# Where GpSimd pauses between scatters, the last tiles of a loop, and four smaller edits in a graph network of four layers

## The chip, the cores and the metric

The kernel runs on one NeuronCore of a Trainium2 chip. The metric is the device time of one execution in microseconds (us). Three executions of the kernel before took 2736.61, 2769.08 and 2771.64 us, median 2769.08. The profiled execution took 2730.27 us, with a span of 2728.6 us from the first to the last instruction.

## The reference, cut to what matters

3125 nodes with 256 features, 103125 edges sorted by target node. Four graph layers follow one another, each on the layer norm of the sum so far:

```python
h = relu(layernorm(x)); x = x + L0(h)   # out-degree scaled sums over src of t1[src] + (feat[src]*feat[dst]) @ W2, then norm
h = relu(layernorm(x)); x = x + L1(h)   # weighted, normalised adjacency, then a 2-layer MLP
h = relu(layernorm(x)); x = x + L2(h)   # undirected adjacency, then a norm over all nodes
h = relu(layernorm(x)); x = x + L3(h)   # attention with 4 heads, softmax over the edges of a target
```

All four use the same edges. So the kernel first builds dense matrices of 25 by 25 blocks of 128 by 128 cells: in one the number of edges between two nodes, in the other their summed weight.

## The kernel before

**Edges.** Each of the 806 columns of an edge list of 128 by 806 is written by one indirect DMA of GpSimd (L378, a scatter of 128 cells) into `table` in HBM. Two edges that fall on the same cell must be merged first. VectorE and TensorE do this in `dedupe(c)` for a batch of 128 columns at a time, seven batches (0 to 6); a batch runs eight passes of an equality test (L452), a weighting (L458) and matmuls with an identity that sum them (L800). The code of every batch is written out; it is not shared between batches. Between batch 1 and batch 2 the same two engines count degrees: `onehot` (L534 to L538) and `degrees` in a loop of 31 groups. Scatter c waits for its batch (`cols`), and the first 160 for the clearing of the part of `table` that they fall in. From scatter 304 (`CALM`) on, a memset of GpSimd on 128 columns of `rest` (L377) stands in front of each scatter.

**L0 and L1's gathering.** When all seven batches are done, 25 steps follow (`step`, L585, L751, L871), one per tile of 128 target nodes. SyncE loads the tile's cells from `table` (L333) once the scatters that fall in it are done (`need`, `done`), TensorE turns and multiplies them, VectorE and ScalarE finish the tile's L0 and its L1 contribution. `overlapped` (L71) orders the steps: tile 0 by itself, then a hardware loop (`Fori`) whose body holds two steps, then the last tiles written out: for the last but three `step` as in the loop, for the last but two without turning the next tile (`more=False`), for the last but one with the earlier tile's gathering ahead of its own loads (`ahead=True`), and the last. L624 runs once in each step.

**L1's rest and L2.** `phase_l12` first does L1's MLP. Then it goes over seven groups `g` of target tiles: 4, 4, 4, 4, 4, 4 and 1. Each group has five parts of 20 matmuls (L1180, shown as L1098); a matmul is as wide as the group's columns: 512, or 54 for the last group.

**L3.** `l3_fast` starts with three `Exp` on ScalarE (L1882 to L1884), the first behind a table load. TensorE spreads two rows with 28 matmuls (L1977), ScalarE copies each row (L1888), VectorE starts once both are there (L1952). GpSimd scales the 25 tiles of `ftx` (L1876), and TensorE's first pass waits for each. The rest of the kernel is L3's eight passes (L2015).

**At the start** five loads bring `src`, `dst` and `dst` shifted by 1, 64 and 512 edges; `extremes` (L419) runs behind batch 0's passes.

Of the kernel before, what the change touches and what calls it, by code (L numbers as in the profile page):

```python
# [37 lines left out]
CALM = 304  # L38
# [32 lines left out]
def overlapped(eng, step):  # L71

    assert NT % 2
    m = NT // 2
    step((0, 0, 0), None)
    with eng.Fori(0, m - 2) as i:
        step((2 * i + 1, 1, i), (2 * i, 0))
        step((2 * i + 2, 0, i + 1), (2 * i + 1, 1))
    step((NT - 4, 1, m - 2), (NT - 5, 0))
    step((NT - 3, 0, m - 1), (NT - 4, 1), more=False)  # L80
    step((NT - 2, 1, m - 1), (NT - 3, 0), ahead=True)
    step((NT - 1, 0, m), (NT - 2, 1), last=True)
    step(None, (NT - 1, 0))
# [101 lines left out]
def phase_edges_and_l0(nc, sem, sb, a):  # L185
# [7 lines left out]
    with ctx:  # L193
# [3 lines left out]
        def pieces(flat, *shapes):  # L197
# [18 lines left out]
        srci, dsti, dst1, dst64, dst512, key, fl, sent, red = pieces(  # L216
            region[:, :, :].rearrange("p a n -> p (a n)"), (I32, EC), (I32, EC), (I32, EC), (I32, EC), (I32, EC),
            (F32, EC), (F32, 3, EC), (F32, EC), (F32, 3, P))
        t0, t1, f0 = fl[:, 0, :].bitcast(I32), fl[:, 1, :].bitcast(I32), fl[:, 2, :]
# [39 lines left out]
        rest = buf("rest", [P, P])  # L259
# [22 lines left out]
        def _(eng):  # L282
            rows = lambda t: t.rearrange("(p c) -> p c", p=P)
            for t, s in ((srci, a.src[0:EP]), (dsti, a.dst[0:EP])):
                eng.dma_start(t, rows(s)).then_inc(sem("ld"), 16)
            for t, s in ((dst1, a.dst[1:EP + 1]), (dst64, a.dst[SH:SH + EP]), (dst512, a.dst[LONG * SH:LONG * SH + EP])):
                eng.dma_start(t, rows(s)).then_inc(sem("ldr"), 16)
# [54 lines left out]
        def _(eng):  # L342
# [20 lines left out]
            late = 20  # L363
            for g in range(NGS):
# [20 lines left out]
        def _(eng):  # L385
# [8 lines left out]
            eng.wait_ge(sem("ldr"), 48)  # L394
# [46 lines left out]
            def dedupe(c):  # L441
# [28 lines left out]
                if c == 0:  # L470
                    extremes()
                if c == 0:
                    eng.wait_ge(sem("ldm"), 64)
# [20 lines left out]
                eng.sem_inc(sem("cols"), 1)  # L494
            dedupe(0)
# [89 lines left out]
            def step(cur, prev, last=False, more=True, ahead=False):  # L585
# [28 lines left out]
                if ahead:  # L614
                    for n in range(13):
                        lift(n)
                    own()
# [15 lines left out]
                if prev and not ahead:  # L633
                    for n in range(5 if last else 13):
                        lift(n)
                if prev and not last and not ahead:
                    own()
# [41 lines left out]
        def _(eng):  # L679
# [71 lines left out]
            def step(cur, prev, last=False, more=True, ahead=False):  # L751
# [6 lines left out]
                if not ahead:  # L758
                    take(k, 3)
                    take(k, 4)  # L760
# [3 lines left out]
                if ahead:  # L764
                    for g in range(5):
                        take(k, g)
# [24 lines left out]
                elif more:  # L791
# [7 lines left out]
        def _(eng):  # L799
# [71 lines left out]
            def step(cur, prev, last=False, more=True, ahead=False):  # L871

                def gathered(chunks):
                    j, z = prev
                    of, g = (wt, g1) if cur else (tk[:, 0, :, :, 1], hk)
                    for n in chunks:
                        eng.wait_ge(sem("af"), 13 * j + max(n + 1, 3))
                        if n < 12:
                            mul = mm(pL[:, n % 3, :], g[:, n % 2 * P:n % 2 * P + P], of[:, 4 * (n // 2):4 * (n // 2) + 4, :], True, True)
                        else:  # L880
                            for o in range(2):
                                mul = mm(pL[:, 0, o * P:o * P + P], g[:, o * P:o * P + P], of[:, NT - 1, :], True, True)
                        mul.then_inc(sem("ag"), 1)
                if ahead:
                    eng.wait_ge(sem("g1"), prev[0] + 1)
                    eng.wait_ge(sem("diag"), prev[0] + 1)
                    gathered(range(13))
                    eng.wait_ge(sem(f"tk{cur[1]}0"), 16 * cur[2] + 16)
                    for g in range(3):
                        turn(cur[0], cur[1], g)  # L890
# [14 lines left out]

                def turn_ab():
# [10 lines left out]
                between = prev and not ahead  # L917
                if between:
# [5 lines left out]
                if between:  # L924
                    gathered(range(0, 3))
                turn_ab()
                if between:
                    gathered(range(3, 5))
                dense()
                if between:  # L930
                    gathered(range(5, 13))
                if more and not last:
# [11 lines left out]
def phase_l12(nc, sem, sb, a, f):  # L944
# [3 lines left out]
    with ExitStack() as ctx:  # L948
# [6 lines left out]
        real = lambda g: min(N, (4 * g + 4) * P) - 4 * g * P  # L955
        rows = lambda t: min(P, N - t * P)
# [34 lines left out]
        def _(eng):  # L991
# [3 lines left out]
            for n in range(NQ * JC):  # L995
                g, j0 = n // JC, JC * (n % JC)
                nt = len(tiles(g))
                if n >= NB:
                    eng.wait_ge(s_("sum"), n - NB + 1)
                for t, d in ((ca, a.counts_b), (cb, a.counts_t)):  # L1000
                    eng.dma_start(t[n % NB][:, 0:nt, :, :].rearrange("p k j d -> p k (j d)"),
                                  d.ap()[4 * g:4 * g + nt, :, j0:j0 + JC, :].rearrange("k p j d -> p k (j d)"))\
# [15 lines left out]
        def _(eng):  # L1018
# [35 lines left out]
            for g in range(NQ):  # L1054
                eng.wait_ge(s_("used"), JC * (g + 1))
                at0 = 4 * g * P
# [1240 lines left out]
```

## Time and profile before

| | us |
|---|---|
| median of three executions | 2769.08 |
| profiled execution, span | 2730.27, 2728.6 |
| TensorE busy, of the span | 1957.7 (72%) |
| VectorE busy | 1341.9 (49%) |
| GpSimd busy | 962.6 (35%) |
| ScalarE busy | 484.0 (18%) |
| the 806 scatters, busy | 810.7 |

An engine is busy while it executes an instruction; issuing and waiting are not counted. Busy shares are means over stages that differ much, so the rows below go by stretches of time. In a row with several stretches, "(x65)" is the number of instructions that fall in the stretch, PEclk the granted TensorE clock (1.00 is 2.4 GHz, 0.50 is 1.2 GHz). "PEld" is TensorE's weight load, and each matmul has one.

### The profile page before, as it was taken

How to read it: one execution, taken by the hardware profiler on the slowest of the kernel's cores; microseconds unless marked ns; L12 is line 12 of the kernel's file. 1: busy time of each engine (PE TensorE's matmuls, PEld its weight loads, DVE VectorE, ACT ScalarE, POOL GpSimd, SP SyncE). 2: the span in 40 equal slices, each digit the busy share in tenths (PEclk: the TensorE clock that was granted, in tenths of full speed). 3: DMA queues.
4: the chain of work that ended last, by engine and by line, in shares of the span. 5: the costliest groups of instructions: out<-in, count | busy, mean ns of one | idle time of the engine just before them, and what ended most of it. 6: DMA issues, size and time to landing. Idle time of an engine off the chain costs nothing. (4 is left out here: it accounts for less than half of the span.)

```text
span 2728.6 us, 22702 instructions
## 1 busy us (share of the span) xinstructions
PE 1957.7 (72%) x7243; PEld 1175.8 (43%) x7253; DVE 1341.9 (49%) x1965; ACT 484.0 (18%) x635; POOL 962.6 (35%) x1346
## 2 busy tenths in 40 slices
PE   4317936243443324248999999989999899999997
PEld 1115822011111213126676777656778634443443
DVE  7345737132332001013545454545664687787886
ACT  0000020000000111104555545443200500000000
POOL 1777874788888887881000000000000130000000
PEclk9755557566665667569999999999998899999998
DMA  7787211000000111205767676732684155565653
GB/s 291 313 337 319 91 57 59 1 7 7 1 1 1 49 49 49 85 13 192 266 220 272 221 271 224 257 145 68 208 263 129 48 163 162 162 184 158 177 174 110
DMA packets 339003, 395.92 MB, mean 145 GB/s; under 512 B 114048, under 2 KB 319722, under 8 KB 325995
## 3 DMA queue, kind: packets, MB, share of 16 engines
q1 hardware_dynamic: 220025, 307.90, 32.2%
q10 hardware_dynamic: 93110, 86.22, 9.7%
q0 software_dynamic: 25792, 0.88, 0.8%
q8 instruction: 37, 0.61, 0.1%
q14 instruction: 39, 0.32, 0.0%
HBM read 222.40 MB, written 172.51 MB: 145 GB/s over the span
## 5 line engine op out<-in xcount | busy, mean ns | idle before, releaser
L378 POOL DMA_INDIRECT table<-valT,idxT x806 | 810.7, 1006 | 275.0 <-issue 246.5
L2015 PE MATMUL psum<-wgt,big 128*65 128x384 f32 (+3 forms) x1600 | 529.3, 492 | 2.4 <-DVE wgt L1965 2.4
L1965 DVE SCALAR_TENSOR_TENSOR wgt<-ratio,l3q,fcj 128x768 f32<-128x768 f32 (+2 forms) x400 | 413.8, 1052 | 99.7 <-PE psum L2015 85.0
L800 PE MATMUL psum<-hx,region 128*128 128x257 f32 x1250 | 317.8, 403 | 146.0 <-issue 111.5
L2015 PEld LDWEIGHTS psum<-wgt,big 128*65 128x65 f32 x1600 | 219.4, 138 | 303.5 <-issue 299.1
L1015 POOL PARTITION_ALL_REDUCE edges<-edge x1 | 0.5, 517 | 923.7 <-DVEq L1384 923.7
L800 PEld LDWEIGHTS psum<-hx,region 128*128 128x128 f32 x1250 | 240.8, 202 | 189.0 <-issue 118.5
L800 PE MATMUL psum<-region,g 128*128 128x512 f32 (+1 forms) x672 | 282.8, 566 | 35.4 <-DVE big L595 19.7
L595 DVE TENSOR_TENSOR big<-big,psum 128x512 f32<-128x512 f32 (+1 forms) x325 | 210.3, 665 | 135.5 <-PE psum L800 93.6
L800 PE MATMUL psum<-big,ident 128*128 128x512 f32 x224 | 154.4, 828 | 129.4 <-issue 104.0
L800 PEld LDWEIGHTS psum<-region,g 128*128 128x128 f32 x672 | 124.9, 196 | 164.5 <-issue 132.9
L800 PE MATMUL psum<-big,identb 128*128 128x512 bf16 x216 | 80.4, 507 | 157.7 <-issue 82.8
L738 ACT ACTIVATE region<-psum 128x512 f32<-128x512 f32 (+1 forms) x175 | 87.0, 549 | 599.1 <-PE psum L868 379.9
L452 DVE TENSOR_TENSOR big<-psum,big 128x2048 bf16<-128x2048 f32 x56 | 127.7, 2290 | 130.5 <-remote 109.1
L800 PE MATMUL psum<-tk,hx 128*128 128x100 bf16 x806 | 146.4, 357 | 57.8 <-DVE tk L538 34.5
L1098 PE MATMUL psum<-l2both,l2z 128*128 128x512 f32 (+1 forms) x700 | 160.4, 392 | 3.3 <-DVE l2z L1273 3.3
L800 PEld LDWEIGHTS psum<-tk,hx 128*128 128x128 bf16 x806 | 116.0, 144 | 88.2 <-DVE tk L538 35.5
L1098 PEld LDWEIGHTS psum<-l2both,l2z 128*128 128x128 f32 x700 | 133.1, 206 | 30.2 <-DVE l2z L1273 4.1
L800 PEld LDWEIGHTS psum<-big,ident 128*128 128x128 f32 x224 | 53.3, 256 | 205.5 <-issue 166.2
L458 DVE TENSOR_TENSOR big<-big,psum 128x1024 f32<-128x1024 bf16 x56 | 67.9, 1215 | 147.4 <-remote 116.7
L1239 DVE TENSOR_TENSOR l2both<-l2m 128x2560 fp32r<-128x2560 bf16 (+1 forms) x35 | 88.9, 2539 | 74.7 <-PE psum L1098 74.5
L800 PEld LDWEIGHTS psum<-big,identb 128*128 128x128 bf16 x224 | 21.5, 115 | 234.5 <-issue 123.0
(216 smaller groups left out, 1676.1 us busy)
## 6 DMA issues: line engine op xcount, KB each, us to landing
table<-tk SPq DMA_DIRECT2D x25, 3200.0 KB
fcj<-counts SPq DMA_DIRECT2D x150, 384.0 KB, 3.5
tk<-table SPq DMA_DIRECT2D x25, 1664.0 KB
counts<-region ACTq DMA_DIRECT2D x25, 1600.0 KB
tk<-table SPq DMA_DIRECT2D x25, 1536.0 KB
fcj<-counts SPq DMA_DIRECT2D x50, 448.0 KB, 3.7
counts_t<-region ACTq DMA_DIRECT2D x25, 800.0 KB
counts_b<-region ACTq DMA_DIRECT2D x25, 800.0 KB
```

Of the source, the lines that this page charges most:

```text
L378: eng.indirect_dma_start(out=table, out_offset=bass.IndirectOffsetOnAxis(idxT[:, c:c + 1], 0), in_=valT[:, c, :], in_offset=None).then_inc ...
L452: eng.tensor_tensor(out, kbp[:, s, :].unsqueeze(1).unsqueeze(1).to_broadcast([P, 2, SB, P]), overlap(win[:, s, :, SB * m:SB * m + P]), ALU ...
L458: eng.tensor_tensor(many(wF[:, m % 2, :]), many(eq[:, m % 2, 0, :]), overlap(ewp[:, s, SB * m:SB * m + P]), ALU.mult).then_inc(sem("we"), 1)
L595: eng.tensor_tensor(part, part, more, ALU.add).then_inc(sem("af"), 1)
L738: eng.activation(cs[:, 4 * g:4 * g + w, :].rearrange("p j d -> p (j d)"), pC[:, g % 3, 0:w * P], ACT.Copy)\
L800: mm = lambda o, l, r_, st, sp: eng.matmul(o, l, r_, start=st, stop=sp, skip_group_check=True)
L1015: eng.partition_all_reduce(f.edges[:, :], f.edge[:, :], P, bass.bass_isa.ReduceOp.max).then_inc(s_("edges"), 1)
L1098: mm = lambda o, l, r_, st, sp: eng.matmul(o, l, r_, start=st, stop=sp, skip_group_check=True)
L1239: eng.tensor_tensor(all_of(both[:, n % 2, :, :, :]), all_of(ca[n % NB]), all_of(cb[n % NB]), ALU.add).then_inc(s_("sum"), 1)
L1965: eng.scalar_tensor_tensor(out=wgt[:, n % NW, u, 0:w], in0=rb[:, 2 * i + u, t0 * P:t0 * P + w], scalar=qs[:, k, 2 * i + u:2 * i + u + 1], ...
L2015: last = eng.matmul(acc[p % 2][u][0:FW, b, 0:hi - lo], ftx[:, k, 2 * i + u, :], wgt[:, n % NW, u, lo:hi], start=k == 0, stop=k == NT - 1, ...
```

## The change

The memsets are of 256 columns instead of 128, and stand in front of scatters 0 to 27 and 112 to 351 (268 in all) instead of 304 to 805 (502). The last four tiles: two of them go through the loop, which makes one more pass, and the last two are as the loop has them; `more` and `ahead` are gone. The four loads of `dst` become one, of overlapping rows of 806 + 512 edges. `extremes` comes ahead of batch 0. The groups of L2 become 4, 4, 4, 4, 3, 3, 3. In L3 the spreading matmuls become transposes, VectorE waits for each of the two rows by itself, VectorE scales the first five tiles of `ftx` and GpSimd the other twenty, and one `Exp` on ScalarE stands at the end of L2.

```diff
-CALM = 304
+FIRST_CODE, LATER_CODE, STEADY = 28, 112, 352
...
     step((0, 0, 0), None)
-    with eng.Fori(0, m - 2) as i:
+    with eng.Fori(0, m - 1) as i:
         step((2 * i + 1, 1, i), (2 * i, 0))
         step((2 * i + 2, 0, i + 1), (2 * i + 1, 1))
-    step((NT - 4, 1, m - 2), (NT - 5, 0))
-    step((NT - 3, 0, m - 1), (NT - 4, 1), more=False)
-    step((NT - 2, 1, m - 1), (NT - 3, 0), ahead=True)
+    step((NT - 2, 1, m - 1), (NT - 3, 0))
     step((NT - 1, 0, m), (NT - 2, 1), last=True)
...
-        rest = buf("rest", [P, P])
+        rest = buf("rest", [P, 2 * P])
...
-            for t, s in ((dst1, a.dst[1:EP + 1]), (dst64, a.dst[SH:SH + EP]), (dst512, a.dst[LONG * SH:LONG * SH + EP])):
-                eng.dma_start(t, rows(s)).then_inc(sem("ldr"), 16)
+            reach = bass.AP(tensor=a.dst.tensor, offset=a.dst.offset, ap=[[EC, P], [1, EC + LONG * SH]])
+            eng.dma_start(ahead[:, 0:EC + LONG * SH], reach).then_inc(sem("ld"), 16)
...
                 for c in range(GS * g, min(EC, GS * g + GS)):
-                    if c > CALM:
-                        eng.wait_ge(sem("rest"), c - CALM)
-                    if c >= CALM:
+                    if c < FIRST_CODE or LATER_CODE <= c < STEADY:
+                        if rests:
+                            eng.wait_ge(sem("rest"), rests)
                         eng.memset(rest[:, :], 0.0).then_inc(sem("rest"), 1)
+                        rests += 1
...
+        first = lambda g: min(4 * g, 3 * g + 4)
+        batch = lambda g: range(first(g), first(g + 1))
...
+            eng.activation(sd[:, 0:1], sd[:, 0:1], ACT.Exp)
...
-            for k in range(NT):
+            for k in range(FIRST, NT):
                 eng.tensor_tensor(ftx[:, k, :, :], ftx[:, k, :, :], e2[:, k, :].unsqueeze(2).to_broadcast([P, H, FW]), ALU.mult)\
...
-                    last = eng.matmul(acc[1][u][:, t // 4, (t % 4) * P:(t % 4 + 1) * P], rr[:, t, H + u:H + u + 1].to_broadcast([P, P]),
-                                      ident[:, :], start=True, stop=True, skip_group_check=True)
+                    last = eng.transpose(acc[1][u][:, t // 4, (t % 4) * P:(t % 4 + 1) * P],
+                                         rr[:, t, H + u:H + u + 1].to_broadcast([P, P]), ident[:, :])
```

## Rows read from the trace of the kernel before

**Rows 1.** The page, 40 equal slices of 68.2 us: busy tenths of GpSimd.
```profile
POOL 1777874788888887881000000000000130000000
```

**Rows 2.** Each engine by stage: stretch, length, us busy (instructions).
```profile
429.80:457.20 27.40, 17.96 (x45) 6.94 (x45) 18.45 (x19) 0.00 (x0) 0.00 (x0) 0.75 0.00 0
457.20:880.00 422.80, 160.94 (x290) 52.48 (x297) 126.41 (x105) 1.84 (x6) 344.51 (x554) 0.62 0.03 4
880.00:1237.00 357.00, 121.59 (x361) 79.09 (x360) 37.55 (x79) 43.58 (x48) 295.25 (x499) 0.63 0.14 47
1237.00:1842.00 605.00, 590.42 (x2489) 423.61 (x2490) 300.21 (x686) 312.55 (x326) 0.00 (x0) 0.99 0.65 233
```

**Rows 3.** Scatters alone (L378): us busy, number, PEclk, DMA share.
```profile
98.50:212.80 114.30, 88.66 (x84) 0.51 0.82 324
212.80:590.60 377.80, 256.90 (x240) 0.59 0.25 91
590.60:1236.50 645.90, 437.81 (x454) 0.62 0.09 27
```

**Rows 4.** All engines (PE, PEld, DVE, ACT, POOL) in three shorter stretches.
```profile
240.00:340.00 100.00, 100.00 (x561) 80.62 (x560) 77.92 (x107) 0.00 (x0) 80.49 (x65) 0.50 0.42 165
460.00:510.00 50.00, 23.52 (x52) 7.19 (x52) 22.70 (x13) 0.33 (x1) 38.12 (x40) 0.70 0.04 5
560.00:660.00 100.00, 40.26 (x67) 12.91 (x67) 28.35 (x19) 0.61 (x2) 84.58 (x143) 0.64 0.04 5
```

**Rows 5.** VectorE by time (start, us): equality tests, batches 1 and 3.
```profile
70.15 2.29 DVE L452 TENSOR_TENSOR big<-psum,big 128x2048 bf16<-128x2048 f32 x1
73.60 2.29 DVE L452 TENSOR_TENSOR big<-psum,big 128x2048 bf16<-128x2048 f32 x1
...
485.63 2.29 DVE L452 TENSOR_TENSOR big<-psum,big 128x2048 bf16<-128x2048 f32 x1 [6.48 <-remote]
507.33 2.29 DVE L452 TENSOR_TENSOR big<-psum,big 128x2048 bf16<-128x2048 f32 x1 [9.98 <-issue]
```

**Rows 6.** L624 alone, one for each tile's step: us busy, their number.
```profile
880.00:1237.00 357.00, 1.45 (x3) 0.63 0.14 47
1245.00:1755.00 510.00, 9.19 (x19) 1.00 0.68 245
1755.00:1824.00 69.00, 1.30 (x3) 0.93 0.52 198
```

**Rows 7.** SyncE in order of time: two successive issues of a tile's load.
```profile
395.63 2.11 SPq L333 DMA_DIRECT2D tk<-table  x2
...
1243.63 0.98 SPq L333 DMA_DIRECT2D tk<-table  x2
```

**Rows 8.** DMA queues, all of 1250:1700 us, one of 470:1230 us.
```profile
q10 hardware_dynamic: 59488, 54.68, 37.8%
q1 hardware_dynamic: 4822, 54.80, 29.8%
...
q14 instruction: 14, 0.11, 0.1%
```

**Rows 9.** GpSimd's memsets in order of time, of 256 and of 128 columns.
```profile
7.55 0.31 POOL L354 MEMSET xs<- 128x256 f32 x1
...
580.81 0.22 POOL L377 MEMSET rest<- 128x128 f32 x1
```

**Rows 10.** L2's matmuls (PE, PEld) in the sixth and in the narrow last group.
```profile
2062.00:2086.00 24.00, 24.00 (x100) 18.52 (x100) 1.00 0.57 185
2086.00:2110.00 24.00, 24.00 (x126) 22.99 (x125) 0.68 0.14 42
```

**Rows 11.** The chain of waits at the start of L3: start, us, what.
```profile
2162.21 1.28 ACT L1882
...
2163.84 6.28 PE psum L1977 x28
```

**Rows 12.** VectorE in order of time behind batch 0's passes.
```profile
52.40 1.22 DVE L421 TENSOR_REDUCE gmm<-tk 101x1 f32<-101x1024 int32 x1 [0.32 <-issue]
```

More of the change, by code:

```diff
@@ L583, in _, with step @@
             begun = ch.n
-            def step(cur, prev, last=False, more=True, ahead=False):
+            def step(cur, prev, last=False):
                 row = lambda t, k: t[:, bass.ds(k, 1), :].rearrange("p a d -> p (a d)")
@@ L632, in step @@
                     itself(tk[:, s, k, :, 1])
-                if prev and not ahead:
+                if prev:
                     for n in range(5 if last else 13):
                         lift(n)
-                if prev and not last and not ahead:
+                if prev and not last:
                     own()
@@ L749, in normal, with step @@
                                bias=ln1[:, 3:4], scale=ln1[:, 2:3]).then_inc(sem("g1"), 1)
-            def step(cur, prev, last=False, more=True, ahead=False):
+            def step(cur, prev, last=False):
                 if not cur:
@@ L757, in step @@
                     normal(prev[0], g1)
-                if not ahead:
-                    take(k, 3)
-                    take(k, 4)
+                take(k, 3)
+                take(k, 4)
                 if prev:
@@ L790, in step @@
                     normal(k, hk)
-                elif more:
+                else:
                     for g in range(3):
@@ L869, in turn, with step @@
                 last.then_inc(sem("tc"), 1)
[L871 to L890, printed above, removed]
+            def step(cur, prev, last=False):
                 if cur:
@@ L916, in dense @@
                     mul.then_inc(sem("e"), 1)
-                between = prev and not ahead
-                if between:
+                if prev:
                     eng.wait_ge(sem("g1"), prev[0] + 1)
@@ L923, in step @@
                     return
-                if between:
+                if prev:
                     gathered(range(0, 3))
                 turn_ab()
-                if between:
+                if prev:
                     gathered(range(3, 5))
                 dense()
-                if between:
+                if prev:
                     gathered(range(5, 13))
-                if more and not last:
+                if not last:
                     eng.wait_ge(sem(f"tk{1 - s}0"), 16 * (r + s) + 16)
@@ L996, in _ @@
                 g, j0 = n // JC, JC * (n % JC)
-                nt = len(tiles(g))
+                nt = len(batch(g))
                 if n >= NB:
@@ L1175, in _ @@
                 for j in range(JC):
-                    nt = len(tiles(g))
-                    blk = both[:, n % 2, 0:nt, j, :] if nt > 1 else both[:, n % 2, 0, j, 0:cols]
+                    blk = both[:, n % 2, 0:len(batch(g)), j, :]
                     for o in range(2):
@@ L1233, in add @@
             def add(n):
-                nt = len(tiles(n // JC))
+                nt = len(batch(n // JC))
                 eng.wait_ge(s_(f"c{n % NB}"), 32 * (n // NB + 1))
```

63 lines of the change are left out of this document (36 added, 27 removed).

## Prediction

> **What bounds the kernel now.** I read the page's slices first, for where GpSimd is at work, then the busy time by stage, then shorter stretches and the order of time inside the slow ones.
>
> GpSimd scatters in the first 18 slices, to 1237 us, and hardly works after [rows 1]. The stages say what that costs. From 457 to 880 us, in which batches 3 to 6 of the merging run, TensorE and VectorE are busy for 161 and 126 of 423 us; from 880 to 1237 us L0 gets through three tiles, with TensorE busy for 122 of 357 us. Then the scatters stop, and TensorE is busy for 590 of 605 us [rows 2]. The steps show it plainly: three tiles in 357 us beside scatters, then 19 in 510 us, 26.8 us each [rows 6]. So 22 of 25 tiles wait until all scatters are over, though a tile needs only its own, some 32 of 806. That is the thing to explain: 22 x 26.8 = 590 us of L0 stand behind the scatters that could lie beside them.
>
> It isn't a wait for data. Equality tests follow one another by 3.45 us in batch 1, with scatters running, but by 21.7 us in batch 3, ended by "issue" and "remote" [rows 5]: the engine had its operands and no instruction to run. SyncE, which computes nothing, issues two loads within 2.11 us beside scatters and within 0.98 us after them [rows 7]. And when GpSimd pauses for 27 us, 45 matmuls and 19 VectorE instructions pass, where the next 423 us see 290 and 105, four to six times fewer per us [rows 2]. What is slow is the feed of instructions to the other engines, while scatters come fast.
>
> How fast they come matters. A plain scatter takes 50 / 40 = 1.25 us, one with a memset of 128 columns 646 / 454 = 1.42 us on the mean, stalls included [rows 4, 3]. In 240 to 340 us scatters come every 100 / 65 = 1.54 us, since VectorE's work makes each last 1.24 instead of 0.95 us, and there TensorE runs 561 matmuls in 100 us without a gap. With the memset, 67 in 100 us [rows 4]. So the feed recovers somewhere between a mean period of 1.42 and 1.54 us, or else the second cause of that good stretch counts: its code is a loop, and already there. Both are what the change leans on.
>
> **The change, part by part.**
>
> *The memset's size.* 256 columns take 0.31 us and 128 take 0.22 [rows 9], so the mean period with the wide memset is about 1.42 + 0.09 = 1.51 us, within the gap named above. Of the 0.17 us between plain and narrow some are stalls that starved code itself makes (bounds 0.09 and 0.17 for the memset, I take 0.10), so a wide memset costs GpSimd 0.19 us. Bounds on what it does to the feed: nothing (67 matmuls in 100 us stay), or all (a batch in 8 x 3.45 + 8 = 36 us instead of the (880 - 457) / 4 = 106 us of now). I take nearly all, since the narrow memset, with half of the pause, stands beside passes of some (106 - 30) / 8 = 9.5 us (30 us for what a batch does outside its passes) against 21.7 us.
>
> The Trainium skill (SBUF — State Buffer, section SBUF: two separate sides) says that VectorE and GpSimd hold their shared port pair exclusively, each for a whole instruction. By it the wide memsets could also block VectorE, for 268 x 0.31 = 83 us at most by the row's duration; the lengthened scatters of 240 to 340 us agree that the two block each other. I count it in the range only.
>
> *GpSimd's own time.* First 28: 28 x 0.19 = 5 us more. From 28 to 111: unchanged, 114 us [rows 3]. From 112 to 351: now 378 us for 240 scatters; 27 us of that is the wait for batch 2 [rows 2], which goes when the batch comes earlier; 192 scatters gain 0.19 (36 us) and 48 gain 0.09 (4 us): 391 us. From 352: 454 x (1.42 - 0.09) = 604 us instead of 646. With the start at 58 (next part): 58 + 41 + 114 + 391 = 604 us for scatter 352, 1208 us for the end of the scatters, 28 us earlier than now. Alone that is 1%.
>
> *What runs beside them.* Batch 2 starts near 400 us now, since batch 1 and the degree loop's first pass had been starved; the first 28 memsets should give back 0 to 70 us of it, I take 35: 366 us. Batches 1 and 2 and the loop between them otherwise keep their lengths. Five batches of 36 us end at 546 us; tile 0 and the first pass of the loop are three tiles, 3 x 27 = 81 us: 627 us, some 23 us behind scatter 352. From there the code of the L0 loop is in place. The loop in [rows 8] fetches nothing: from 1250 to 1700 us only the data queues q10 and q1 move anything, while from 470 to 1230 us q14 fetched instructions 14 times. I take it that such a loop runs beside plain scatters as the degree loop does. Tile 24's L624 then comes 21 x 26.8 = 563 us on at 1190 us, or with 10% for the company of the scatters at 1246 us. The last scatters, at 1208 us, plus one load and one turning (some 35 us), give 1243 us. The two limits meet at 1246 us, where this L624 now comes at 1824 us, the end of the last stretch of [rows 6]. That is -578 us. Cover gone: with L0 beside the scatters nothing hides the scatters any more, so they become the bound of the stage.
>
> *Last tiles in the loop.* Three L624 took 69 us in the written-out order against 54 in the loop [rows 6]: -15 us where L0 is bound by work. Where tiles wait for scatters, `ahead` was useful, and dropping it costs up to 15. I set 0 with the overlap, -15 without.
>
> *L2's groups.* The sixth group takes 24 us for 100 matmuls. The narrow one takes nearly as long, 23.5, at a clock that falls to 0.68 [rows 10]. Six wide and a narrow one: 6 x 24.3 + 23.5 = 169 us; four wide and three of 384 columns, each bounded by weight loads (100 x 0.19 us) plus the change of group (2): 97 + 63 = 160 us. -9 us; bounds 0 and -16.
>
> *L3's start.* The table load, 1.28 us, moves under VectorE's tail of L2: -1.3. The 28 spreading matmuls took 6.28 us on the chain [rows 11]; as transposes they should take about half, and VectorE waits for the first row alone: -4.5. VectorE's five scalings fit ahead of that row, but push its first products by up to 1. Sum -5, bounds 0 and -7.
>
> *The start.* One load of overlapping rows for four and both reductions of `extremes` (two of 1.22 us [rows 12]) off the chain to scatter 0: -5 us, bounds 0 and -8; it counts only as far as scatters bound what follows.
>
> **Sum.** -578 (start and scatters in it) - 9 - 5 = -592 on the profiled 2730: 2138 us. The profiled run lies 39 us below the median of three, whose spread (35 us) is as wide; I add the 39 and a little for a first loop pass that is still starved: **2190 us**.
>
> **The rivals.**
>
> *Released only in part (0.16).* The feed starves loops as well as new code. For: SyncE's load code is a loop. The Trainium skill (Runtime: NRT & Kernel Launch, section Instruction fetch mechanics) has a rule on that side: a taken branch whose target lies outside the window that was fetched forces a new fetch first. That no fetch shows in 1250 to 1700 us speaks against it for L0's loop. Then from 352 on, without memsets, a tile takes 200 us or so (119 us now, and passes lengthen from 9.5 to 22 us without memsets), so up to three more tiles pass beyond the first three: 20.5 +- 1.5 tiles stand behind the scatters, against 22 now. With the scatters' 28 us that is -68 us, and with L2 and L3 -82: 2690 us with the 39 added. That is at the edge of 2%.
>
> *Slower (0.12).* A pause of 0.09 us more does nothing for the feed, and the memsets end at scatter 352 while new code is still being run. Then batch 4 is under way at 632 us, and 2.5 batches follow at 22 us a pass, 206 us each: L0 starts at 1150 us, so no tile lies beside the scatters. All 25 stand behind: 3 x 26.8 = +80 us, and the scatters end 3 us later. Less 14 of the small parts and with the 39: 2840 us. It decides from the point where batch 6 ends after 880 us.
>
> *Little happens (0.14).* The wide memset doesn't reach the feed's threshold, and the gains behind 352 and the losses before it offset each other: 2740 us. That the memsets don't reach the other engines' feed at all, the change not doing what it says, lies here and in the case above.
>
> **How the numbers follow.** Released: 0.58, 2190 us, its own range 2110 to 2430 (loop steps of 26.8 to 36 us, L2 and the start at their bounds). The 80% range takes in that case, most of the second and the lower part of the fourth: 2110 to 2730. Two per cent is 55 us, about what a measurement of this kernel can tell from no change, so the limits are 2714 and 2824. Faster: 0.58 + half of 0.16 + 0.02 = 0.68. Slower: 0.12. Within: 0.20.
>
> **What would show it.** Right: equality tests 3.5 to 4 us apart in batches 2 to 6, batch 6 over before 620 us; L624 evenly spaced from 650 us; few tiles behind the last scatter; TensorE busy over 80% in 650 to 1200 us. Wrong at the first step: passes of 9 us or more beside wide memsets. Wrong at the second: batches fast, but L624 100 us or more apart after scatter 352. Scatters with wide memsets at a period other than 1.45 to 1.5 us would move the 604 us. L2: seven groups that sum to 169 us or more would show its part wrong; for L3 the first product should start 5 us after the first `Exp`.

## The result and the profile after

The changed kernel takes 2634.28 us (median of 4 runs, 2630.78 to 2637.88). The kernel before, run again beside it, takes 2756.11. The ratio is 0.9605, 95% interval 0.955 to 0.966: 4% faster, where 2190 us, 20% faster, was forecast. In the profiled executions the span fell from 2728.6 to 2628.8 us, by 99.8 us.

The page of the kernel after, 40 slices of 65.7 us, is the counterpart of [rows 1]:

```profile
PE   5599477773211122113999999999998999999996
...
DVE  7878588231000000002454545555665878787886
...
POOL 2888888887777777772000000000000400000000
PEclk9755798886555555555999999999999999999998
```

VectorE used to be half starved up to slice 13. Now its merging is over in slice 8, and from slice 10 it stands nearly still for nine slices, in which only GpSimd is at work throughout. The hole has not closed: it has moved from the merging to L0. The busy times by stage, as in [rows 2] (stretch, length, then PE, PEld, DVE, ACT, POOL, clock, DMA share, GB/s):

```profile
288.00:468.00 180.00, 138.43 (x366) 50.51 (x374) 155.30 (x132) 3.36 (x10) 158.64 (x247) 0.88 0.14 47
468.00:596.00 128.00, 100.38 (x389) 71.68 (x387) 37.66 (x80) 49.75 (x53) 109.84 (x170) 0.89 0.41 141
596.00:1212.00 616.00, 110.16 (x231) 61.44 (x230) 28.17 (x63) 29.44 (x30) 458.87 (x454) 0.55 0.10 29
1212.00:1769.00 557.00, 537.83 (x2251) 382.64 (x2251) 280.15 (x635) 275.74 (x290) 0.00 (x0) 0.98 0.61 219
```

Five batches now take 180 us, 36 us each, with VectorE busy for 155 of them. L0 starts at once, at a good pace. At 596 us the memsets stop, and from there 231 matmuls run in 616 us, against 389 in the 128 us before. TensorE, mostly idle there, is granted a clock of 0.55 on the mean: most of that stretch is at the lower level, 1.2 GHz. L0's q instruction (L617, L624 before), one for each tile, tells it in tiles, as in [rows 6]:

```profile
486.00:597.00 111.00, 1.94 (x4) 0.91 0.49 164
597.00:1240.00 643.00, 0.97 (x2) 0.55 0.10 29
1250.00:1741.00 491.00, 9.19 (x19) 1.00 0.67 243
```

Four tiles in 111 us beside scatters with wide memsets (35 us from one to the next on the mean), two in 643 us beside plain ones (294 and 322 us from one to the next), then 19 at 26.8 us each. The loop's body holds two tiles, so the two slow ones, tiles 4 and 5, run code that tiles 2 and 1 had run before. GpSimd around scatter 352 (start, us, idle before in brackets):

```profile
592.73 0.96 POOL L377 DMA_INDIRECT table<-valT,idxT  x1 [0.17 <-issue]
593.70 0.33 POOL L375 MEMSET rest<- 128x256 f32 x1
594.19 0.96 POOL L377 DMA_INDIRECT table<-valT,idxT  x1 [0.17 <-issue]
595.45 0.96 POOL L377 DMA_INDIRECT table<-valT,idxT  x1 [0.30 <-issue]
596.72 0.96 POOL L377 DMA_INDIRECT table<-valT,idxT  x1 [0.30 <-issue]
```

With the memset a scatter comes every 1.46 us (594.19 - 592.73), plain every 1.26. Some 0.19 us for each scatter is all that the memset costs GpSimd, and all that separates 35 us a tile from 300. SyncE's two load issues, as in [rows 7], just before the memsets stop and inside the plain stretch:

```profile
592.20 1.60 SPq L331 DMA_DIRECT2D tk<-table  x2
...
791.47 4.20 SPq L331 DMA_DIRECT2D tk<-table  x2
```

SyncE's code is a loop that had run before, and it computes nothing. Of its 11 instructions between 784 and 797 us most lie 0.70 or 1.40 us apart, and after 1250 us most lie 0.06 to 0.1 us apart. So loops starve too.

By stage the 99.8 us are: the first matmul of L1's rest and L2 comes 84.0 us earlier (1853.2 to 1769.2), L1's rest and L2 are 11.5 us shorter (305.3 to 293.8), and from there to L3's first product it is 4.9 us less (12.6 to 7.7). L3 itself is unchanged to 0.6 us.

### The profile page after: what moved, and what is told of

It is laid out like the page before. It is cut to its first block and busy times, and to the rows that moved or that the text cites. A ratio compares the mean times of both kernels' runs of the same rounds, so it can differ in the third digit from the quotient of the medians.

```text
span 2628.8 us, 22584 instructions
## 1 busy us (share of the span) xinstructions
PE 1912.9 (73%) x7229; PEld 1164.1 (44%) x7239; DVE 1340.5 (51%) x1970; ACT 483.5 (18%) x636; POOL 955.0 (36%) x1107
## 5 line engine op out<-in xcount | busy, mean ns | idle before, releaser
L377 POOL DMA_INDIRECT table<-valT,idxT x806 | 831.0, 1031 | 227.8 <-issue 227.2
L789 PE MATMUL psum<-region,g 128*128 128x512 f32 (+1 forms) x672 | 297.7, 586 | 103.1 <-issue 59.2
L617 DVE TENSOR_SCALAR q<-psum,rso 128x256 f32<-128x256 f32 x25 | 12.1, 484 | 312.6 <-remote 236.2
L1084 PE MATMUL psum<-l2both,l2z 128*128 128x512 f32 (+1 forms) x700 | 147.8, 372 | 3.3 <-DVE l2z L1258 3.3
L595 DVE TENSOR_TENSOR region<-region,ident 128x128 f32 (+1 forms) x24 | 7.1, 295 | 249.1 <-ACT region L755 176.0
L1224 DVE TENSOR_TENSOR l2both<-l2m 128x2560 fp32r<-128x2560 bf16 (+1 forms) x35 | 88.8, 2539 | 65.5 <-PE psum L1084 65.2
L789 PE MATMUL psum<-big,ident 128*128 128x512 f32 x224 | 112.0, 629 | 3.4 <-issue 0.6
L857 PE MATMUL psum<-ident,tk 128*128 128x128 f32 x625 | 101.5, 295 | 17.8 <-issue 17.2
L789 PE MATMUL psum<-big,identb 128*128 128x512 bf16 x216 | 68.1, 442 | 59.7 <-DVE big L450 52.6
```

The costliest lines, as they stand in the source:

```text
L595: eng.tensor_tensor(w, w, ident[:, :], ALU.add).then_inc(sem("diag"), 1)
L617: do(eng.tensor_scalar(q[:, :], pq[:, 0:D], one(rso), None, ALU.mult))
L789: mm = lambda o, l, r_, st, sp: eng.matmul(o, l, r_, start=st, stop=sp, skip_group_check=True)
L857: last = eng.transpose(pC[:, g % 3, o:o + P], tk[:, s, j, :, 0], ident[:, :])
L1084: mm = lambda o, l, r_, st, sp: eng.matmul(o, l, r_, start=st, stop=sp, skip_group_check=True)
L1224: eng.tensor_tensor(all_of(both[:, n % 2, :, :, :]), all_of(ca[n % NB]), all_of(cb[n % NB]), ALU.add).then_inc(s_("sum"), 1)
```

## The experiments

**The question.** Theory: every engine's instructions, loops included, stop coming when scatters come faster than about 1.45 us apart. Rival: the memsets help code that is fetched for the first time, and the L0 loop is slow for another reason. All edits are to the changed kernel unless said otherwise.

**e1, wide memsets to the end.**

```
-                    if c < FIRST_CODE or LATER_CODE <= c < STEADY:
+                    if c < FIRST_CODE or LATER_CODE <= c:
```

> The changed kernel, with the memset of 256 columns also in front of every scatter from 352 to the end. Theory (the instruction feed of all engines, loops included, starves beside scatters that come every 1.26 us and not beside ones every 1.45 us): L0's tiles, which now come 300 us apart from scatter 352 on, come as fast as the scatters allow, 32 x 1.455 = 47 us apart or faster, the scatters end at 595 + 454 x 1.48 = 1267 us, the last tile's q at about 1300 us where it now stands at 1740: about 2634 - 440 = 2195 us. Rival (a looping code runs or starves for a reason of its own, the memsets help only code that is fetched): tiles stay about 300 us apart until the scatters end, which is 85 us later: about 2720 us.

Measured: 2210.62 us, ratio to before 0.813 (0.8076 to 0.8183). L0's q's lie 28 to 39 us apart from 572 to 1101 us, then four times 46 to 55 us, where they wait for scatters; the last one comes at 1326 us, the last scatter at 1282. Its page:

```profile
DVE  7977678854433434344332235656567777878885
...
POOL 1888788888788788788888810000004000000000
```

The hole is gone, and the time of the released case is there, though by a kernel that was not the one predicted. The theory holds, the rival falls. The feed is not wholly free: up to 1101 us these tiles are 33 us apart on the mean.

**e2, e8 and e18: how long must the pause be?** 128, 192 and 224 columns from scatter 352 on. The edit of e2, the others with another width:

```
-                    if c < FIRST_CODE or LATER_CODE <= c < STEADY:
+                    if c < FIRST_CODE or LATER_CODE <= c:
...
-                        eng.memset(rest[:, :], 0.0).then_inc(sem("rest"), 1)
+                        eng.memset(rest[:, 0:P if c >= STEADY else 2 * P], 0.0).then_inc(sem("rest"), 1)
```

> The changed kernel, with a memset of 128 columns in front of every scatter from 352 to the end (256 columns stay in the old places). It asks where between a period of 1.26 and 1.45 us the feed recovers. Theory: partly; at the 119 us a tile that the kernel before showed beside the same memsets, (1225 - 596) / 119 = 5 tiles pass where now 2 do, 16 remain behind the scatters, which end 25 us later: 2634 - 3 x 27 + 25 = about 2580 us. If 1.36 us is enough for the loop: about 2195 us. Rival (the memsets do nothing for a loop): about 2660 us.

> The changed kernel with memsets of 192 columns in front of every scatter from 352 to the end. Scatters by themselves would come every 1.41 us, between the 1.36 us of 128 columns, beside which tiles came 95 to 160 us apart, and the 1.455 us of 256, beside which they came 31 us apart. Theory (the feed recovers steadily with the length of each pause): tiles 45 to 60 us apart, 2250 to 2350 us. If the feed recovers at a threshold below 1.41 us: as fast or faster than with 256 columns, since the scatters end some 20 us earlier: about 2190 us.

> The changed kernel with memsets of 224 columns in front of every scatter from 352 to the end, evenly spread, a period of 1.43 us. Four together in front of every eighth made the same mean period, 1.434 us, and 2457 us. On a chip that starves: if the mean period decides, tiles come 70 us apart and it takes about 2440 us; if each gap's length decides, with a threshold between the 1.40 us of 192 columns (2494 us) and the 1.455 us of 256 (2211 us), either end is possible, and a time below 2350 us would show that spreading helps. On a chip that does not starve: about 2190 us.

**e7 and e16: one long pause instead of many short ones.** Eight, or four, memsets of 256 columns in front of every eighth scatter from 352 on:

```
+                    for _ in range(1 if c < FIRST_CODE or LATER_CODE <= c < STEADY else 8 if c >= STEADY and c % 8 == 0 else 0):
```

> The changed kernel with eight memsets of 256 columns together in front of every eighth scatter from 352 on: the mean period is near the 1.5 us of the kernel with one in front of each, but seven of eight scatters follow at 1.26 us. If the mean period decides (a backlog that has to drain): tiles 30 to 45 us apart, about 2200 us. If each gap decides (the feed moves at a full pace only in the pause behind a scatter): one part in four of the time is a pause in which it moves fast, tiles come some 80 to 120 us apart, 6 or 7 pass before the scatters end near 1290 us, and the time is about 2600 us.

> The changed kernel with four memsets of 256 columns together in front of every eighth scatter from 352 on. Eight of them made a step of 4.03 us beside seven of 1.26, so four should make one of 2.66: a mean period of (7 x 1.263 + 2.66) / 8 = 1.44 us. Theory (something serves the scatters and the feed in turn, needs about 1.40 us for a scatter, as SyncE's instructions 1.40 us apart beside plain scatters suggest, and only what the mean period leaves over goes to the feed): a little is left over, so tiles come 35 to 60 us apart, about 2200 to 2320 us. Rival (evenly spread pauses are needed, and eight together only worked because the pause was long): tiles 100 us or more apart, 2450 us or more.

> The changed kernel with four memsets of 256 columns together in front of every eighth scatter from 352 on, a mean period of 1.436 us. On a chip that starves: if the mean period decides and a scatter needs about 1.40 us of whatever also serves the feed, tiles come 35 to 60 us apart, 2200 to 2320 us; if evenly spread pauses are needed, tiles come 100 us or more apart, 2450 us or more. On a chip that does not starve: 2185 us, as before.

e9 told nothing of this, for a reason that comes below; e16 is the same kernel once more, on another chip. The L617 rows of 610 to 1020 us in the kernel after, e2, e8, e18, e1, e16 and e7 (the number in brackets is that of the tiles):

```profile
610.00:1020.00 410.00, 0.48 (x1) 0.54 0.07 17
```
```profile
610.00:1020.00 410.00, 1.45 (x3) 0.58 0.14 47
```
```profile
610.00:1020.00 410.00, 1.94 (x4) 0.67 0.21 70
```
```profile
610.00:1020.00 410.00, 3.39 (x7) 0.83 0.38 131
```
```profile
610.00:1020.00 410.00, 5.80 (x12) 0.96 0.57 197
```
```profile
610.00:1020.00 410.00, 2.42 (x5) 0.73 0.28 96
```
```profile
610.00:1020.00 410.00, 5.80 (x12) 0.95 0.57 195
```

| from scatter 352 on | usual step, us | scatters in 410 us | tiles in 410 us | time, us | ratio to before, interval |
|---|---|---|---|---|---|
| plain (the kernel after) | 1.26 | 310 | 1 | 2634 | 0.9605 (0.955 to 0.966) |
| 128 columns each (e2) | 1.35 | 294 | 3 | 2539 | 0.9339 (0.9277 to 0.9401) |
| 192 (e8) | 1.40 | 292 | 4 | 2494 | 0.9162 (0.9118 to 0.9205) |
| 224 (e18) | 1.43 | 286 | 7 | 2331 | 0.8546 (0.8512 to 0.8579) |
| 256 (e1) | 1.45 | 273 | 12 | 2211 | 0.813 (0.8076 to 0.8183) |
| four together (e16) | seven of 1.27, one of 2.56: mean 1.43 | 288 | 5 | 2457 | 0.8996 (0.8927 to 0.9065) |
| eight together (e7) | seven of 1.26, one of 4.03: mean 1.61 | 254 | 12 | 2268 | 0.8335 (0.8287 to 0.8383) |

The feed comes back steeply between 1.40 and 1.45 us. e7 shows that not each gap has to be long. e16 and e18 have nearly the same mean step and differ by 126 us, which looks as if spread pauses did better than gathered ones; e18's expectation had named a time under 2350 us as the sign of it. But they are not quite alike: some steps are longer than the usual one, so the third column, the scatters that fall in the same 410 us, is the truer mean. By it all seven kernels stand in one order, the fewer scatters the more tiles, with e16 (288) between e8 (292) and e18 (286). On so steep a curve these two scatters may be the whole difference: the mean step can explain every row, and that spreading helps is not shown.

Several expectations missed: e8 took 2494 us, where its two cases had about 2190 and 2250 to 2350; e16's tiles came 71 us apart, between its cases of 35 to 60 and of 100 or more, though its time is that of the second.

**e3 and e4: size, and none.** e3 has 128 columns in the changed kernel's places, e4 no memsets (`if False:`).

> The changed kernel with memsets of 128 columns in place of 256, in the changed kernel's places. Theory (the size, by the period that it makes, is what sped up batches 2 to 6): passes go back to about 9.5 us beside it, the batches to some 80 to 106 us each, the last of them ends near 850 us, behind scatter 352 even slower, L0 starts at about 900 us or later: 2740 us or more. Rival (the place, the first 28 and 112 on, did it): batches stay at 36 us, and the time at 2634 - 25 = 2610 us.

> The changed kernel without any memset between the scatters. Theory: passes of 12 to 33 us beside plain scatters at 1.26 us, batches of about 200 us each, GpSimd waits for the addresses of several batches, L0 stands whole behind the scatters: 2850 us or more. Rival (the memsets' port conflict slows VectorE more than the pause helps): about the changed kernel's time or less.

e3: 2725.40 us, ratio 1.0032 (1.0004 to 1.006). e4: 2744.09 us, 1.0086 (1.0046 to 1.0126). Equality tests by time in e3, where plain scatters have set in, and in e4:

```profile
623.84 2.29 DVE L450 TENSOR_TENSOR big<-psum,big 128x2048 bf16<-128x2048 f32 x1 [9.98 <-issue]
646.24 2.29 DVE L450 TENSOR_TENSOR big<-psum,big 128x2048 bf16<-128x2048 f32 x1 [9.98 <-remote]
```
```profile
630.02 2.29 DVE L450 TENSOR_TENSOR big<-psum,big 128x2048 bf16<-128x2048 f32 x1 [9.98 <-remote]
652.43 2.29 DVE L450 TENSOR_TENSOR big<-psum,big 128x2048 bf16<-128x2048 f32 x1 [9.99 <-remote]
```

A starved pass takes 22.4 us beside plain scatters, in both kernels. Size made the difference in the end: with the small size the changed places bring no gain in time, as expected, though e3 has the small parts' help too. At the start the small size was enough: e3's batch 2 begins at 303 us (409 in the kernel before), and loses its lead in the batches after it. Even without any memset the time is only 0.9% over that of the kernel before, again with the small parts' help. e4 was expected at 2850 or more: GpSimd waits three times for addresses, 75 us in all, and I had not counted what passes in them: 45 matmuls in the first, of 27 us, against 109 in the 199 us behind it.

**e5, the memsets alone.** The kernel before with only the changed kernel's memsets:

```
-                    if c > CALM:
-                        eng.wait_ge(sem("rest"), c - CALM)
-                    if c >= CALM:
+                    if c < 28 or 112 <= c < 352:
+                        if rests:
+                            eng.wait_ge(sem("rest"), rests)
                         eng.memset(rest[:, :], 0.0).then_inc(sem("rest"), 1)
+                        rests += 1
```

> The kernel before, with the memsets alone changed (256 columns, in front of the first 28 scatters and of 112 to 351); the other parts of the change are left undone. Theory: the traces give L2's groups 11.5 us and L3's start 4.9 us of the 100 us by which the profiled span fell, and L0's stage the other 84; of these the memsets make about 65 to 80 and the last tiles in the loop and the start the rest. So this kernel stands at 2634 + 16 + 5 to 20 = 2655 to 2670 us, and its batches 2 to 6 take 36 us each as in the changed kernel. Rival (the start or the looped last tiles carry the gain of L0): 2700 us or more.

Measured: 2637.50 us, ratio 0.9691 (0.9647 to 0.9735), against 0.9605 for the whole. In its trace L2's first matmul comes at 1763.4 us, 6 us earlier than in the changed kernel: three tiles, not two, passed in the stretch of plain scatters, and the written-out last tiles give 16 of those 22 us back. L2 (303.7 us) and L3's start (12.2) are as before. So the memsets made most of L0's gain, and L2 and L3 the rest.

**e6, e10 and e15: what about a scatter starves the feed?** e6 puts three memsets in place of each scatter from 352 on. e10 and e15 are one kernel, run on two chips, in which the scatters from 352 on write half of their rows:

```
+                    rows = P // 2 if c >= STEADY else P
-                    eng.indirect_dma_start(out=table, out_offset=bass.IndirectOffsetOnAxis(idxT[:, c:c + 1], 0),
-                                           in_=valT[:, c, :], in_offset=None).then_inc(sem(f"scat{g % 2}"), 16)
+                    eng.indirect_dma_start(out=table, out_offset=bass.IndirectOffsetOnAxis(idxT[0:rows, c:c + 1], 0),
+                                           in_=valT[0:rows, c, :], in_offset=None).then_inc(sem(f"scat{g % 2}"), 16)
```

> The changed kernel without the scatters 352 to 805: in place of each stand three memsets of 256 columns, so that GpSimd is kept about as busy (some 1.2 us for each) and issues as many instructions or more, but no indirect DMA. It leaves out the writing of 454 columns of counts, so its time says nothing of the whole. Theory (it is the indirect DMA that starves the feed): L0's tiles come 27 us apart from 490 us on, 25 of them by 1160 us, and the time is 2634 - (1740 - 1140) = about 2040 us. Rival (GpSimd's rate of instructions, or its busy time, starves the others): tiles remain 100 us or more apart until GpSimd is through.

> The changed kernel, with each scatter from 352 on writing 64 of its 128 rows; no memset is added. It leaves out half of those counts, so its time says nothing of the whole. If the work per row is what crowds out the feed (1.40 us for 128 rows, so 0.70 us for 64, well under the period of 1.26 us): L0's tiles come 27 to 32 us apart, about 2040 to 2150 us. If the cost is per scatter, whatever it writes: tiles stay some 300 us apart, about 2630 us, or worse if the scatters then come faster.

> The changed kernel, with each scatter from 352 on writing 64 of its 128 rows, no memset added; it leaves out half of those counts. On a chip that starves: if the work per row crowds out the feed, tiles come 27 to 32 us apart and the time is 2040 to 2150 us; if the cost is per scatter, tiles stay 300 us apart, about 2630 us. On a chip that does not starve it tells nothing: about 2085 us.

e6: 2035.07 us. All engines in its 600 to 1060 us:

```profile
600.00:1060.00 460.00, 460.00 (x1966) 332.45 (x1965) 234.23 (x532) 244.03 (x255) 388.29 (x1247) 1.00 0.68 243
```

GpSimd is busier than with scatters (388 of 460 us, 1247 instructions), and TensorE has not one gap: tiles come every 26.8 us. A busy GpSimd starves nobody; indirect DMAs do. e15: 2630.79 us against 2630.49 for the changed kernel on the same chip. Its scatters usually take 0.90 instead of 0.96 us and come every 1.20, and one tile passes in 410 us:

```profile
610.00:1020.00 410.00, 0.48 (x1) 0.54 0.06 18
```

So it is the scatter as an instruction that costs the feed, not the rows that it writes. Its scatters don't gain either: the last 454 take 608 us in both kernels, because longer steps lie between the short ones. On e10's chip, which is told of next, they take 552 us, against 589 with all rows (e11).

**e11 and e17: without the first 28 memsets.**

```
-                    if c < FIRST_CODE or LATER_CODE <= c < STEADY:
+                    if LATER_CODE <= c < STEADY:
```

> The changed kernel without the memsets in front of the first 28 scatters. Theory (they pace the scatters while batch 1 and the first pass of the degree loop fetch their code, and that is what brought batch 2 from about 400 to 288 us): batch 2 starts 40 to 100 us later, the batches end near 530 us instead of 468, two or three tiles fewer lie ahead of scatter 352: 2634 + 2.5 x 27 = about 2700 us. Rival (the first 28 do little, the stretch from 112 on does it all): batch 2 starts within 15 us of where it does now, 2620 to 2645 us.

> The changed kernel without the memsets in front of the first 28 scatters. On a chip that starves, theory (they pace the scatters while batch 1 and the first pass of the degree loop fetch their code): batch 2 starts 40 us or more later than at 288 us, two or three tiles fewer lie ahead of scatter 352, about 2690 us. Rival (the stretch from 112 on does it all): batch 2 starts within 15 us of 288 us, 2620 to 2645 us. On a chip that does not starve: 2121 us, as before.

e11 took 2121.50 us, and the kernel before, on the same chip, 2127.48 (2125.2 to 2131.1, 10 runs), where it had 2720 to 2756 in the five other sets of runs. No feed starves in e11's trace, and plain scatters every 1.26 us are no hindrance there. L617 and all engines in e11, and SyncE's two issues beside plain scatters:

```profile
610.00:1020.00 410.00, 6.77 (x14) 0.96 0.64 225
```
```profile
600.00:1150.00 550.00, 483.90 (x2034) 353.69 (x2033) 237.24 (x545) 253.03 (x268) 409.72 (x424) 0.93 0.59 208
```
```profile
667.75 0.89 SPq L331 DMA_DIRECT2D tk<-table  x2
```

Four kernels ran on that chip (e9 to e12) and all four went so. So the starving hangs on the chip, or on its state at that time, and the kernel only sets it off. e17, on a chip that starves, took 2686.46 us, ratio 0.9853 (0.9823 to 0.9884), as the theory had it. All engines in 103 to 208 us, in e17 and in the kernel after:

```profile
103.00:208.00 105.00, 15.40 (x68) 9.64 (x68) 32.24 (x38) 0.00 (x0) 82.00 (x76) 0.50 0.83 329
```
```profile
103.00:208.00 105.00, 93.33 (x523) 75.32 (x524) 83.48 (x113) 0.00 (x0) 84.88 (x67) 0.50 0.81 325
```

In both, scatters 28 to 111 are plain. In e17 76 of them come in 105 us, one every 1.38; in the kernel after 67 come, one every 1.57. What stands still in e17 is the end of batch 1 and the degree loop's first pass. The loop's own instruction (L531, one for each of the 31 groups), in e17 before and after 209.8 us, where GpSimd's step is 7.7 us long and the wide memsets begin, and then in the kernel after:

```profile
150.00:208.00 58.00, 5.64 (x3) 0.50 0.82 326
208.00:268.00 60.00, 21.48 (x12) 0.50 0.83 335
```
```profile
103.00:150.00 47.00, 17.03 (x9) 0.50 0.78 315
150.00:208.00 58.00, 22.74 (x13) 0.50 0.83 333
```

In the kernel after the groups come 4.6 to 5.2 us apart from the loop's first pass on, beside plain scatters. So code that runs for the first time goes well there, and the same code stands still in e17. The likely reason is that the first 28 memsets got the engines going, and from then on VectorE's own work stretches the scatters (1.24 us each) and so keeps the feed open. The kernel before and e4 show the other way in: their degree loop too starts late (181 and 175 us), and goes at full pace only behind a step of GpSimd of 8.3 and 7.4 us (at 213 and 208 us), with no memset near. That the stretching keeps it going is argued from the steps and was not tried by itself. Batch 2 starts at 288 us in the kernel after and at 381 in e17.

**e12, e13 and e14.** e12 is the kernel before with e1's memsets, e13 and e14 are the two kernels once more.

> The kernel before with the memset of 256 columns in front of the first 28 scatters and of all from 112 to the end, the other parts of the change left undone (the last tiles written out, L2's groups, L3's start, the loads at the start). Against the changed kernel with the same memsets, 2211 us: L2 and L3 take 15 us more; the last tiles wait for scatters there, 47 to 54 us apart, so the written-out order, which takes the gathering of a tile ahead, neither gains nor loses more than 15 us; the start is 4 us later: 2215 to 2245 us. Rival (the looped last tiles cost time where they wait for scatters): 2195 to 2210 us, no slower than the kernel with all parts.

> The kernel before, unchanged, for its trace on this chip. If the chip is one that starves the feed: 2720 to 2760 us, L0's first q behind 900 us, tiles 100 us apart beside the scatters. If not: about 2127 us, passes of the equality tests 3.5 us apart and tiles 26.8 us apart, both beside scatters at 1.35 us, and the stage ends with the last scatters near 1240 us.

> The changed kernel, unchanged. On a chip that starves: 2634 us, 0.96 of before. On one that does not: the L0 stage is bound by the scatters, which end at 1185 to 1190 us with plain ones from 352 on, against about 1215 us with the narrow memsets of before: 25 to 30 us less, and 16 us from L2 and L3, less what the looped last tiles lose: about 2127 - 25 - 16 = 2085 us to 2120 us, the upper end being what the kernel without the first 28 memsets took, 2121 us.

e14: 2630.49 us, ratio 0.9626 (0.9585 to 0.9667); e13: 2733.24, 0.9997 (0.9966 to 1.0028). The result repeats on another chip. e12 ran on the chip without starving: 2213.60 us, ratio 1.0399 (1.0381 to 1.0418). The same memsets that go with a saving of 19% on one chip (e1, which has the small parts too, some 20 us) cost 4% on the other: GpSimd's last scatter comes at 1273 us there, against 1185 in e11, and L0's end follows it. Beside it e9 took 2184.62 us and e10 2084.77, and neither could tell its two cases apart, since nothing starved. From 512 to 862 us e12's tiles come 26.8 to 27.9 us apart, beside the memsets that e1 has, where e1's come 33 us apart: so what e1 still lacks is the starving's too. Whether looped last tiles cost time where they wait for scatters stays open, since e12 had no counterpart on its chip.

## Why the prediction failed

**The diagnosis held.** The feed of instructions starves beside fast scatters: e1, e2, e8 and e18 move one width and the tiles follow. It lacked two things: it is the DMA and not GpSimd's work (e6), and it needs a chip that does it (e11). One of its readings was wrong: in GpSimd's pause of 27 us in [rows 2] there pass 1.64 matmuls and 0.69 VectorE instructions per us, in the 423 us after it 0.69 and 0.25, so 2.4 and 2.8 times fewer, and not four to six.

**First step, the wide memset frees new code: right.** Passes are 3.45 us apart, with the batches at 36 us as forecast. Batch 4 in the kernel after, to be read against batch 3 in [rows 5]:

```profile
365.10 2.29 DVE L450 TENSOR_TENSOR big<-psum,big 128x2048 bf16<-128x2048 f32 x1
...
368.55 2.29 DVE L450 TENSOR_TENSOR big<-psum,big 128x2048 bf16<-128x2048 f32 x1
```

The memset costs GpSimd 0.19 us, as forecast. The end of batch 6 came at 468 us, not 546: I gave the first 28 memsets 35 us, with 70 as the bound, and by e17 they are worth 93 in the start of batch 2 (381 to 288). Scatter 352 came at 595.5 us for 604 and the last one at 1203 for 1208, and that was in part luck: scatters 28 to 111 took 133 us for 114, beside a degree loop at full pace, and 112 to 351 took 360 for 391.

The range held 83 us for memsets that block VectorE. Equality tests beside wide memsets keep their 2.29 us and their step of 3.45, so no such cost shows here. The Trainium skill (SBUF — State Buffer, section SBUF: two separate sides) has VectorE and GpSimd lock their shared ports for a whole instruction, but of VectorE's instructions it names only those in a two-port mode, and those with two SBUF inputs beside a GpSimd instruction that reads SBUF; a memset reads nothing, and the prediction had left this condition out.

**Second step, L0's loop beside plain scatters runs like the degree loop: wrong, and the whole miss.** It carried -578 us; L0's stage gave -84. Beside plain scatters its tiles came 294 and 322 us apart, where I had 26.8 plus at most 10%. I had two explanations for the good stretch in [rows 4], a mean step of 1.54 us or code in place, and built on the second for L0. The second is refuted in the kernel after itself: tiles 4 and 5 starve in code that is in place, and its degree loop goes at full pace in its first pass, when the code is not. The first fits all runs: VectorE's work lengthens the scatters beside the degree loop (1.24 us), the work of L0 hardly does (0.97 us on the mean in e11, with L0 at full pace), and L0's loop recovers when memsets bring the step to 1.45 us (e1). The row against me was in the text too: SyncE's load code, a loop, took 2.11 us for two issues beside scatters [rows 7]. I gave it to a rival at 0.16. That the queues of [rows 8] show no fetch for the L0 loop was right and proves nothing, since no more transfers of code go with starving than without it. Between 620 and 1190 us, with L0 starved in the kernel after and at full pace in e11, q14 fetches four times in each:

```profile
q14 instruction: 4, 0.03, 0.0%
```
```profile
q14 instruction: 4, 0.03, 0.0%
```

The Trainium skill (Runtime: NRT & Kernel Launch, section Instruction fetch mechanics) would have a taken branch pay for a new fetch where its target lies outside the window that was fetched. These equal counts speak against that as the cause.

**Which case it was.** "Released only in part", with plain scatters starving the loop. It had 20.5 +- 1.5 tiles behind the scatters and 2690 us. 19 q's lie behind 1250 us, and it took 2634. Of the 56 us between, 35 come from the 39 us that I added from the profiled execution to the median: of the changed kernel the median lies 4 us above its profiled time, and later runs gave the kernel before medians of 2720 to 2739 on chips that starve, near its profiled 2730. The other 21 are mostly batches that ended 78 us sooner than I had them, so that four tiles and not three passed early; a tile beside plain scatters took 300 us where I had 200.

**The small parts: right.** L1's rest and L2 gave -11.5 for a forecast of -9. A group of 384 columns takes 17.5 us for its 100 matmuls, where I had bounded it by weight loads at 19, and a wide one 24, as in [rows 10]:

```profile
1960.00:1977.50 17.50, 17.50 (x101) 17.37 (x101) 9.88 (x7) 0.12 (x1) 0.00 (x0) 1.00 0.72 226
1979.00:1996.50 17.50, 17.50 (x100) 17.12 (x99) 10.18 (x7) 0.00 (x0) 0.00 (x0) 1.00 0.78 253
```

L3's start gave -4.9 for -5, with the table load now on ScalarE while VectorE closes L2, and 14 transposes in 3.25 us for the 28 matmuls in 6.28 of [rows 11], of which the first product waits for one half:

```profile
2063.50 1.28 ACT L1080 ACT_TABLE_LOAD   x1
...
2067.63 3.25 PE L1965 MATMUL psum<-ident,small 128*128 128x128 f32 x14 [4.64 <-ACT small L1867]
...
2070.74 2.28 DVE L1953 SCALAR_TENSOR_TENSOR wgt<-ratio,l3q,fcj 128x896 f32<-128x896 f32 x2 [0.99 <-DMA fcj<-counts]
```

That product now waits for the load of `fcj`, which ended 0.99 us of idle time: what is late next there. The looped last tiles gave -15.8 without overlap (two steps in 53.6 us for e5's 69.4), for the -15 that I had set for that case. The start gave -3.8 (scatter 0 at 58.8 for 62.6).

## What to carry to other kernels

When a stretch runs well where its neighbour starves, and two causes would explain it, price the change by each of them, and don't build on the one that suits. Look at an engine that computes nothing (here SyncE) to tell a starved feed from a wait for data, and measure the kernel before on more than one chip before its bottleneck is tuned: the pauses that go with a gain of 19% where the feed starves lose 4% where it doesn't.

## What the runs showed of the hardware

- In five of six sets of runs, indirect DMAs from GpSimd with a usual step of 1.26 us starve the other engines, whether their code is new or a loop: SyncE's instructions from 784 to 797 us mostly lie 0.70 or 1.40 us apart, and TensorE, which had 389 matmuls in 128 us, has 231 in 616. At 1.45 us apart they run nearly freely (33 us a tile against 26.8 in e6), at 1.40 they do not. Half the rows change nothing (e15), memsets at the same rate do not starve anyone (e6).
- One set of six showed none of it, with the same kernel before at 2127 instead of 2720 to 2756 us. What differs in that chip, or in its state, no run here shows, and it can't be read from the kernel.
- In that case the scatters do bound L0, as the prediction had it for a released loop: from 912 to 1203 us e11's q's come 34 to 52 us apart, and its median is 0.3% under that of the kernel before (0.9954 to 0.9977). The whole change was not run on such a chip.
